# Setup transfers of a one-core fused kernel in a new order and on other queues

## The reference

```python
p = patches of x: (32, 14*14, 768)             # 16x16x3
y = layernorm(p) * ln1_g + ln1_b
y = y @ W + bias                               # W: 768x256
h = concat([layernorm(y) * ln2_g + ln2_b, txt], axis=1)      # 32 x 273 x 256
x_sub = rmsnorm(layernorm(h)[:, ::2]) * g_norm
x_proj, gate = split(x_sub @ w_in.T + b_in)
state = tanh(state * A + x_t * Bm); y_t = state @ Cm.sum(0) + Dv * x_t     # scan over time
h = h + repeat((ys * silu(gate)) @ w_out.T + b_out, 2)
h = h + ffn(layernorm(h))       # silu(x @ w_gate.T) * (x @ w_up.T) @ w_down.T, int32 weights / 127
```

## Time and profile before

| | us |
|---|---|
| median of three executions | 1236.9 |
| lowest and highest | 1234.11 and 1238.8 |
| the profiled execution | 1238.44 |
| its span in the trace | 1236.6 |

### The profile page before, as it was taken

One profiled execution on the slowest core, in us unless ns is written; L12 is line 12 of the kernel. 1 busy time (PEld: TensorE's weight loads), 2 busy tenths in 40 slices (PEclk: granted clock), 3 DMA queues, 4 the chain that ended last, 5 costly groups with the idle time before them and its releaser, 6 DMA issues.

```text
span 1236.6 us, 25959 instructions
## 1 busy us (share of the span) xinstructions
PE 1179.6 (95%) x7257; PEld 647.2 (52%) x7257; DVE 1057.5 (86%) x2390; ACT 953.6 (77%) x1891; POOL 393.7 (32%) x384
## 2 busy tenths in 40 slices
PE   6898999999999999999999999999999999999977
PEld 4652556565656565555555555554544544545435
DVE  5978989898989898989898989887998999888933
ACT  2377797979797979797979797878879888897842
POOL 5312242434343333333333333323222222321220
PEclk8989999999999999999999999999999999999999
DMA  9133232323232424242424242213322323323110
GB/s 244 37 84 90 60 98 69 98 66 99 64 100 63 101 62 103 60 105 59 107 56 111 53 113 50 75 45 84 105 76 77 97 65 104 78 72 93 41 38 25
DMA packets 154819, 99.80 MB, mean 81 GB/s; under 512 B 129072, under 2 KB 143536, under 8 KB 153424
## 3 DMA queue, kind: packets, MB, share of 16 engines
q1 hardware_dynamic: 151120, 97.58, 31.6%
q10 hardware_dynamic: 3648, 1.58, 0.6%
HBM read 58.52 MB, written 40.60 MB: 80 GB/s over the span
## 4 chain that ended last, share of the span: by engine, by line
PE 71%; DVE 13%; ACT 6%; issue 6%; DMA 1%; SPq 1%; POOL 0%; ACTq 0%; DVEq 0%; POOLq 0%
PE Y L1446 14%; PE U L1436 14%; PE P L1507 8%; PE P L1611 7%; PE P L1612 7%; PE P L1542 4%; PE P L1627 4%; PE P L1628 4%; DVE U L867 4%; PE P L1492 3%; PE P L1562 3%; ACT y_fx L1221 2%; ACT h L1134 2%; DVE act L1018 1%; DVE fx_split L1024 1%
## 5 line engine op out<-in xcount | busy, mean ns | idle before, releaser
L867 DVE TENSOR_TENSOR U<-h,a_col 128x512 f32<-128x512 f32 x1096 | 711.3, 690 | 90.5 <-ACT h L1134 84.3
L1134 ACT ACTIVATE h<-U 128x512 f32<-128x512 f32 x1096 | 610.5, 609 | 171.7 <-PE U L1436 166.4
L1436 PE MATMUL U<-x_diag,b_st 128*128 128x512 f16 x1096 | 352.8, 382 | 10.1 <-DVE U L867 7.1
L1446 PE MATMUL Y<-h,read_st 128*32 128x512 f32 x2192 | 266.2, 604 | 0.6 <-ACT h L1134 0.4
L1436 PEld LDWEIGHTS U<-x_diag,b_st 128*128 128x128 f16 x1096 | 100.4, 99 | 177.4 <-DVE U L867 120.6
L1355 POOL TENSOR_TENSOR xT_act<-act,xT_act 128x448 f16<-128x448 f32 x114 | 118.3, 1041 | 185.2 <-ACT xT_act L1241 185.2
L1507 PE MATMUL P<-tok_w,xT_act 128*112 128x256 f32 x648 | 155.1, 380 | 0.0
L1507 PEld LDWEIGHTS P<-tok_w,xT_act 128*112 128x112 f32 x648 | 114.8, 178 | 28.9 <-ACT xT_act L1154 0.3
L1446 PEld LDWEIGHTS Y<-h,read_st 128*32 128x32 f32 x2192 | 57.4, 109 | 131.3 <-issue 113.5
L1627 PE MATMUL P<-down_w,xT_act 128*112 128x256 bf16 (+1 forms) x480 | 115.5, 276 | 2.1 <-DVE xT_act L1038 1.4
L1628 PE MATMUL P<-down_w,xT_act 128*112 128x256 bf16 (+1 forms) x480 | 114.9, 275 | 0.0
(11 more groups left out here) (169 smaller groups left out, 1374.5 us busy)
## 6 DMA issues: line engine op xcount, KB each, us to landing
raw<-in_x SPq DMA_DIRECT2D x42, 448.0 KB, 6.4
gate_scr<-gate_o SPq DMA_DIRECT2D x20, 448.0 KB, 2.5
gate_in<-gate_scr SPq DMA_DIRECT2D x20, 448.0 KB, 7.8
tok_scr<-tok SPq DMA_DIRECT2D x19, 448.0 KB, 3.1
res<-tok_scr SPq DMA_DIRECT2D x19, 448.0 KB, 3.8
out<-outs SPq DMA_DIRECT2D x76, 112.0 KB, 2.7
x_diag<-scan_scr SPq DMA_DIRECT2D x312, 16.0 KB
x_diag<-scan_scr SPq DMA_DIRECT2D x304, 12.0 KB
```

Source lines behind the costliest of these rows:

```text
L867: dve.tensor_tensor(U[bank_of(slot)][:, :].rearrange("p (l b) -> p l b", b=B), h[:, (slot - CHUNKS) % RING, :].rearrange("p (l b) -> p l b ...
L1134: sc.activation(h[:, slot % RING, :], U[bank_of(slot)][:, :], ACT.Tanh, scale=1.0 / U_SCALE).then_inc(squashed, 1)
L1436: pe.matmul(U[bank_of(slot)][:, :], b_st[:, c, :], x_diag[:, c, :, t * B:t * B + B], start=False, stop=True, skip_group_check=True).then_i ...
L1446: mm = pe.matmul(Y[c4 * 32:c4 * 32 + 32, :], read_st[:, t, half, :], h[:, (t * CHUNKS + half * RG + c4) % RING, :], start=(t == 0 and half ...
```

## The change

Nothing that computes is moved, added or taken away. Only transfers move, with their semaphores:

- SyncE issues `W` ahead of the images instead of behind them.
- ScalarE issues `g1`, `b1`, `cst` in this order; before it was `cst`, `b1`, `g1`. `g1` has a semaphore of its own, s_gain, for which `gain_mean` waits; `bias_part` waits for `b1` alone.
- The seven transfers that ScalarE issued after a wait for the images (`w_in`, `A`, `w_out`, three for `cols`, `read_st`) are issued by SyncE behind `b_out`, with no wait.
- SyncE's wait for s_wts (48), ahead of the integer weights, is gone.

```diff
         def setup_sync(sp):
+            sp.dma_start(w_st, W.rearrange("(h k c) e -> k h c e", h=2, c=CH)).then_inc(s_w, 16)
             load_raw(sp, 0)
-            sp.dma_start(w_st, W.rearrange("(h k c) e -> k h c e", h=2, c=CH)).then_inc(s_w, 16)
...
-            sp.wait_ge(s_wts, 48)
-            sp.sem_inc(passed, 1)
+            sp.dma_start(w_in_r, w_in.rearrange("(k p) d -> p k d", p=128)).then_inc(s_wts, 16)
...
         def setup_scalar(sc):
+            sc.dma_start(g1, ln1_g.rearrange("(h k c) -> k h c", h=2, c=CH)).then_inc(s_gain, 16)
+            sc.dma_start(b1, ln1_b.rearrange("(h k c) -> k h c", h=2, c=CH)).then_inc(s_gb, 16)
             sc.dma_start(cst[:, 0:C_READ], consts[:, 0:C_READ]).then_inc(s_cst, 16)
...
-            sc.wait_ge(raw_in, CH * 16)
-            sc.dma_start(w_in_r, w_in.rearrange("(k p) d -> p k d", p=128)).then_inc(s_wts, 16)
...
         def gain_mean(dve):
-            dve.wait_ge(s_gb, 32)
+            dve.wait_ge(s_gain, 16)
...
         def bias_part(pe, f):
...
-                pe.wait_ge(s_gb, 32)
+                pe.wait_ge(s_gb, 16)
```

More of the change, by code:

```diff
@@ L325, in build @@
         s_gb = sem("s_gb")
+        s_gain = sem("s_gain")
         s_cread = sem("s_cread")
@@ L394, in setup_sync @@
             sp.dma_start(rows[:, 3, :], b_out.rearrange("(a d) -> a d", a=1).to_broadcast([PT, D])).then_inc(s_rows, 16)
-            sp.wait_ge(s_wts, 48)
-            sp.sem_inc(passed, 1)
+            sp.dma_start(w_in_r, w_in.rearrange("(k p) d -> p k d", p=128)).then_inc(s_wts, 16)
+            sp.dma_start(a_r, A.rearrange("(p two) s -> p (two s)", two=2)).then_inc(s_wts, 16)
+            sp.dma_start(w_out_r, w_out.rearrange("(k p) d -> p k d", p=128)).then_inc(s_wts, 16)
+            for c0, v in ((6, g_norm), (0, b_in), (4, Dv)):
+                sp.dma_start(cols[:, c0:c0 + v.shape[0] // 128], v.rearrange("(k p) -> p k", p=128),
+                             allow_slow_non_contiguous=True).then_inc(s_cols, 16)
+            sp.dma_start(read_st[:, :, :, :].rearrange("p t k m -> p (t k m)"), consts[:, C_READ:C_COLS]).then_inc(s_cread, 16)
             for where, w, k0, n in ffn_r:
@@ L408, in setup_scalar @@
         def setup_scalar(sc):
+            sc.dma_start(g1, ln1_g.rearrange("(h k c) -> k h c", h=2, c=CH)).then_inc(s_gain, 16)
+            sc.dma_start(b1, ln1_b.rearrange("(h k c) -> k h c", h=2, c=CH)).then_inc(s_gb, 16)
             sc.dma_start(cst[:, 0:C_READ], consts[:, 0:C_READ]).then_inc(s_cst, 16)
-            sc.dma_start(b1, ln1_b.rearrange("(h k c) -> k h c", h=2, c=CH)).then_inc(s_gb, 16)
-            sc.dma_start(g1, ln1_g.rearrange("(h k c) -> k h c", h=2, c=CH)).then_inc(s_gb, 16)
             sc.wait_ge(s_half, 1)
             sc.activation(fsg[:, 0, 0:1], half_th[:, :], ACT.Silu).then_inc(passed, 1)
-            sc.wait_ge(raw_in, CH * 16)
-            sc.dma_start(w_in_r, w_in.rearrange("(k p) d -> p k d", p=128)).then_inc(s_wts, 16)
[L416 to L421, removed]
         def setup_vector(dve):
```

## The result

| | before | after |
|---|---|---|
| median, us | 1238.27 | 1241.07 |
| span of the profiled execution | 1236.6 | 1239.2 |

The ratio of the paired executions is 1.0031 with a 95% interval of 1.0018 to 1.0044: 0.3% slower, clear of no change, and within the 0.5% that I had named as hard to tell. In us the ratio is 3.8, the difference of the medians 2.8, that of the two spans 2.6. One of the seven executions of before took 1498.34 us; it counts in the median and, as a slow one, not in the ratio, and without it the medians differ by 3.5. Forecast were 1238.6 in a range of 1234.5 to 1243.

A forecast was written before the change was run, and what follows sets the result against it. The prediction took the chain of waits in early setup, through column_mean and bias_part to bias_add, as the bound. With cst deciding, column_mean ends at 22.45 instead of 20.74: 1236.9 + 1.7 = 1238.6 us, range 1234.5 to 1243.

The forecast's parts named there:

- +1.7 us: Shift of setup and the scan behind it: column_mean was to end at 22.45 instead of 20.74 us.
- cst is starved: Rival, 12%: ScalarE's third transfer waits for SyncE's stream; cst lands at 16.3, shift 5.0 us, total 1241.9.
- What bounds: Start of setup: a chain of waits, not busy time; column_mean, bias_part, then bias_add; each us is 0.08%.
- Moves the rest of setup by the same amount: Setup behind column_mean: whatever moves its end moves bias_part, the rest of setup and the scan by the same amount.
- Images behind W, +2.3: Start of SyncE's queue: images land 2.3 us later, at about 13.3; bounds +1.0 to +3.2.
- cst at 13.0: ScalarE's queue: cst behind g1 and b1 lands at 13.0 instead of 6.74 us; the three transfers together took until 13.8.
- The decision point: TensorE ahead of column_mean: cst landing before 11.65 us is hidden by the images, each us after is paid in full.
- the images decide: Rival, 20%: cst lands before about 10, TensorE idles, column_mean runs 18.5 to 23.0; shift +2.3 us, total 1239.2.
- The clock at column_mean, -1.9: column_mean: with the idle stretch gone, 12 matmuls take 2.6 us at high clock instead of 4.51; gain up to 1.9.
- the scan gives nothing back: Behind setup: the scan, which TensorE fills, was to recover none of the shift.
- Nothing for the seven transfers: Seven transfers moved to SyncE, integer weights and images of group 1 requested sooner: sum 0; 1.56 us if cover were gone.

The follow-up runs named there:

- e8: The kernel of e5 with gain_mean as DVE's first work, ahead of the 13 patch statistics; run 0.9972 of the kernel before.
- e1: The changed kernel with cst first again on ScalarE's queue, ahead of g1 and b1; run 1.0024 of the kernel before.
- e3: The kernel before with only ScalarE's first three transfers reordered to g1, b1, cst; run 1.0000 of the kernel before.
- e2: The changed kernel with the images ahead of W again, cst still third; run 0.9995 of the kernel before.
- e5: The changed kernel with TensorE's wait for cst moved from its first instruction to bias_part, transfers untouched; run 1.0002 of the kernel before.
- e4: The kernel before with only the seven transfers moved to SyncE behind b_out and SyncE's wait for them gone; run 0.9986 of the kernel before.
- e9: The kernel of e8 with the images ahead of W; run 0.9961 of the kernel before.
- e10: The kernel of e9 with 16 filler matmuls instead of 24; run 0.9971 of the kernel before.

## Why the prediction was right, and where it wasn't

**The size.** The forecast rests on +1.7 us; measured were 2.8 to 3.8. The 1241.07 us are nearer to the 1241.9 of the rival "cst is starved" than to the forecast's 1238.6, but cst landed at 13.9 and not at the rival's 16.3, and 1.4 us of the distance lie in the median of before, 1238.27 now instead of 1236.9.

**What bounds.** That bias_add hangs on the end of column_mean held: in all kernels but e8 column_mean, bias_part and bias_add follow one another with no gap. "Moves the rest of setup by the same amount" held within half a us for a later bias_add: +2.8 there, +3.2 at the clearing (59.43 against 56.24). For an earlier one it failed: in the second and third profile of before bias_add is 1.7 and 2.7 us ahead of the first, the clearing only 1.1 and 0.8.

**Images behind W, +2.3.** Measured +1.5 and +1.6. The step failed by its bytes: I kept cst's 240 KB beside the images, but by its new place it went behind them, which I had only as the lower value of +1.0. e1, where cst shares the start, has +2.5. W alone landed at 5.6, and bought nothing, as said; e8 shows what it buys when gain_mean is moved.

**cst at 13.0.** Measured 13.96 and 14.03. Close to the 13.8 of the sum of the three transfers, from which I had taken off 0.8 for W's smaller packets. That reason doesn't hold: g1 took 5.3 us behind W's packets and 4.9 behind the images' (e3).
**The decision point.** cst was later than 11.65, so cst decided, as forecast. Kernel e1 is the rival "the images decide": forecast +2.3 to bias_add with the slow clock, measured +3.0, the 12 matmuls taking 5.46 us instead of 4.5.

**The clock at column_mean, -1.9.** In the changed kernel it was what I expected: clock 1.00, 2.6 us. The error is on the other side. I took the 4.51 us of one execution of before for a property of the kernel. In two of three profiles it is 2.83, and then there is nothing to win. Against the mean of the three, with bias_add at 22.0, the two profiles of the changed kernel (26.5 on average) are 4.5 us late there, and 4.1 at the clearing (59.7 against 55.6). This is the term that was mis-sized most: about -0.6 instead of -1.9, if one in three executions has the slow column_mean.

**What happened behind the setup.** I said that the scan gives nothing back. It gave and took. At the token statistics of the next group the changed kernel is 0.9 us late in the first pair of profiles (84.32 against 83.38), having been 3.2 late at the clearing. Between 62 and 90 us, the line of before:

```profile
62.00:90.00 28.00, 25.18 (x133) 14.67 (x130) 21.69 (x58) 21.84 (x41) 4.49 (x5) 0.88 0.40 93
```

and of after:

```profile
62.00:90.00 28.00, 24.24 (x141) 13.41 (x139) 23.73 (x67) 21.16 (x39) 6.64 (x7) 1.00 0.44 100
```

The kernel before has its stretch of low clock there (0.88, 0.88 and 0.82 in three profiles), the changed kernel none (1.00 twice). Later the changed kernel loses again. One place is in the loop, between 850 and 875 us; there before has

```profile
850.00:875.00 25.00, 23.05 (x156) 10.91 (x154) 21.58 (x39) 18.66 (x38) 5.67 (x6) 1.00 0.36 92
```

and after

```profile
850.00:875.00 25.00, 23.05 (x142) 10.94 (x140) 19.91 (x33) 17.80 (x36) 5.46 (x6) 0.93 0.34 86
```

From ScalarE's copy of Y in this group to that in the next (L1138; L1140 before) it took 50.3 us instead of 48.7 (859.72 to 910.01, against 858.39 to 907.05). So 1.6 us came from a low clock in a loop whose TensorE is busy in 23.05 of 25 us in both. It is in both profiles of the changed kernel, in none of the three of before, but also in e2 to e5 and in e8, whose runs are as fast as before or faster. The sum of all this left about 3 us of the 4 in the spans. That the total is no further from the forecast's +1.7 is partly luck, the work of stretches that the forecast didn't price.

**Nothing for the seven transfers.** Held for the changed kernel, where the images of group 1 are there long before their use: POOL sorts them at 33.09, and DVE's first step on the tokens comes at 42.08. It doesn't hold for the kernel before as two of its three profiles show it. There these images come last, and their earlier issue is worth about 0.5 us (e4). The prediction named this path, with 1.56 us of waiting, and took it as covered.

**What stays open.** Why q10's small pieces get through fast when the images are first on the other queue and slowly when W is. Why the low clock in the loop comes where it comes, and whether the change has a part in it. And how often the kernel before has its slow column_mean: three profiles are no measure of a frequency.

## What to carry to other kernels

Loading something earlier is worth nothing while its reader stands behind another wait on its engine; and what was moved back to make room can be what an engine waits for first, so look at the first wait of every engine (here e5: one misplaced wait, 3.7 us, or 2.0 without the high clock that came with it). What looks free in one profile can be the next bound: here the images of group 1, once bias_add came earlier. Price a clock term only from more than one profile of the kernel before: a slow stretch beside a short idle time can be a matter of the single execution. Small scattered transfers ahead of one that is waited for cost far more than their bytes: the same 3 KB took 6.6 us or 11.6 us, by the order on the other queue.

## What was not expected of the hardware

- gain_mean, 128x6 elements, took 0.15 us when it came after POOL's two sorting copies (14.25 to 16.05). When it met one of them it took 0.20 to 0.89 us and ended at 15.09 to 15.10 or at 16.07 to 16.10, about as a copy did. In e8, issued shortly before POOL's long clearing, its record is 8.37 us long and ends at 14.33, with POOL's at 14.31:

```profile
5.96 8.37 DVE L435 TENSOR_SCALAR x_diag<-x_diag 128x6 f32<-128x6 f32 x1 [4.78 <-DMA x_diag<-in_L_tok_ln_g]
...
6.74 7.57 POOL L517 MEMSET x_diag<- 128x8960 int32 x1
```

In e9 and e10, where it started at 5.37 and 5.81, it ended at 6.83, with POOL's first clearing at 6.80. So in e8 it was this that released column_mean at 14.48, 0.7 us after the filler. What ties the two engines was not tried.

- A stretch of 1.2 GHz in the steady loop costs 1.6 us and shows no idle time ahead of it that the other kernel hasn't; two or three of these are as much as the whole effect of this change.
